# Scaling softmax probabilities on GpSimd instead of scaling the attention's output

## The reference, cut to what matters

```python
def attention(q, k, v, mask):
    scores = jnp.einsum('bhqd,bhkd->bhqk', q, k) / jnp.sqrt(jnp.float32(HD))
    scores = scores * mask - 10000.0 * (1.0 - mask)
    probs = jax.nn.softmax(scores, axis=-1)
    return jnp.einsum('bhqk,bhkd->bhqd', probs, v)
```

## Time and profile before

| What | Value |
|---|---|
| Median of 3 runs | 1197.53 us |
| The profiled execution's own time | 1199.37 us |
| Its span | 1197.6 us |
| TensorE busy (matmuls) | 1178.5 us, 98% |
| VectorE busy | 942.7 us, 79% |
| ScalarE busy | 849.1 us, 71% |
| GpSimd busy | 608.6 us, 51% |
| Granted TensorE clock, mean | 0.997 |

### The profile page before, as it was taken

One profiled execution on the slowest core, in us unless ns is written; L12 is line 12 of the kernel. 1 busy time (PEld: TensorE's weight loads), 2 busy tenths in 40 slices (PEclk: granted clock), 3 DMA queues, 4 the chain that ended last, 5 costly groups with the idle time before them and its releaser, 6 DMA issues.

```text
span 1197.6 us, 35319 instructions
## 1 busy us (share of the span) xinstructions
PE 1178.5 (98%) x13184; PEld 974.1 (81%) x13184; DVE 942.7 (79%) x2298; ACT 849.1 (71%) x2277; POOL 608.6 (51%) x1003
## 2 busy tenths in 40 slices
PE   9999999999999999999999999999999999999998
PEld 8778788787887878788788887878888787888877
DVE  4787887978788697787978788697887879779764
ACT  4777687767867778686767877677786786866543
POOL 3554664646455463654646455473654645363341
PEclk8999999999999999999999999999999999999999
DMA  8401000100100000010000100000000100000000
GB/s 238 142 33 31 2 24 1 31 2 16 33 6 27 5 14 19 11 30 5 24 1 2 44 6 23 8 15 2 22 28 2 31 13 6 8 6 2 1 7 10
DMA packets 27623, 27.91 MB, mean 23 GB/s; under 512 B 11072, under 2 KB 25408, under 8 KB 26816
## 3 DMA queue, kind: packets, MB, share of 16 engines
q1 hardware_dynamic: 26240, 24.99, 6.9%
q10 hardware_dynamic: 1216, 0.66, 0.3%
HBM read 23.53 MB, written 2.10 MB: 21 GB/s over the span
## 4 chain that ended last, share of the span: by engine, by line
PE 88%; DVE 4%; issue 3%; POOL 2%; ACT 2%; DMA 1%; SPq 0%; POOLq 0%; DVEq 0%; ACTq 0%
PE bank L659 10%; PE bank L539 9%; PE bank L932 9%; PE attended L614 9%; PE bank L942 9%; PE bank L599 9%; PE bank L694 6%; PE bank L665 5%; PE bank L720 4%; PE bank L683 4%; PE bank L707 4%; PE bank L652 3%; PE bank L510 2%; PE bank L433 2%; PE bank L711 2%
## 5 line engine op out<-in xcount | busy, mean ns | idle before, releaser
L586 POOL TENSOR_SCALAR p_a<-p_a,rec_a 128x256 f32<-128x256 f32 x512 | 245.9, 498 | 93.2 <-DVE rec_a L560 92.7
L575 ACT ACTIVATE p_a<-bank,nmax_a 128x256 f32<-128x256 f32 x512 | 237.6, 475 | 67.9 <-DVE nmax_a L554 66.8
L554 DVE TENSOR_REDUCE nmax_a<-bank 128x2 f32<-128x512 f32 x256 | 170.5, 680 | 24.0 <-PE bank L539 23.0
L599 PE MATMUL bank<-ident,p_a 128*128 128x128 f32 x1024 | 142.2, 274 | 0.3
L539 PE MATMUL bank<-cc,q_a 64*128 64x256 f32 x1024 | 133.4, 391 | 1.1 <-issue 0.2
L599 PEld LDWEIGHTS bank<-ident,p_a 128*128 128x128 f32 x1024 | 117.0, 141 | 13.2 <-issue 8.0
L614 PE MATMUL attended<-p_a,v_a 128*64 128x256 f32 x1024 | 125.2, 386 | 0.0
L539 PEld LDWEIGHTS bank<-cc,q_a 64*128 64x128 f32 x1024 | 94.7, 186 | 29.1 <-issue 15.2
L575 ACT ACTIVATION_READ_ACCUMULATOR p_a<-bank,nmax_a 128x1 f32 x512 | 104.9, 205 | 0.0
L614 PEld LDWEIGHTS attended<-p_a,v_a 128*64 128x64 f32 x1024 | 67.4, 136 | 41.5 <-issue 11.3
L632 DVE COPY p_a<-bank 128x512 f32<-128x512 f32 x128 | 86.3, 679 | 6.2 <-PE bank L599 5.5
(11 more groups left out here) (265 smaller groups left out, 2855.4 us busy)
## 6 DMA issues: line engine op xcount, KB each, us to landing
xx<-in_x SPq DMA_DIRECT2D x32, 128.0 KB, 3.0
cc<-in_ctx SPq DMA_DIRECT2D x32, 128.0 KB, 2.9
wc<-in_wc SPq DMA_DIRECT2D x3, 1024.0 KB, 7.3
k_c<-in_ctx SPq DMA_DIRECT2D x16, 128.0 KB, 2.3
wb<-in_wb SPq DMA_DIRECT2D x2, 1024.0 KB, 8.5
res_a<-in_x SPq DMA_DIRECT2D x16, 128.0 KB, 2.1
out<-y_out SPq DMA_DIRECT2D x16, 128.0 KB, 1.7
wb<-in_wb SPq DMA_DIRECT2D x2, 512.0 KB, 5.8
```

The costliest lines, as they stand in the source:

```text
L554: dve.tensor_reduce(nmax_a[:, n, e, :], ps[:, :].rearrange("p (q k) -> p q k", q=KT), AX.X, ALU.max, negate=True).then_inc(A.s["max"], 1)
L575: last = act.activation(p_a[:, j % 2, n, e, qt, :], ps[:, qt * D:(qt + 1) * D], ACT.Exp, bias=nmax_a[:, n, e, qt:qt + 1], accum_out=sum_a[ ...
L586: last = pool.tensor_scalar(p_a[:, j % 2, n, e, qt, :], p_a[:, j % 2, n, e, qt, :], rec_a[:, n, e, qt:qt + 1], 1.0, ALU.mult, ALU.mult)
L599: last = nc.tensor.transpose(ps[:, kt * D + qt * P:kt * D + (qt + 1) * P], p_a[:, j % 2, n, e, qt, kt * P:(kt + 1) * P], ident[:, :])
```

## The change

The reciprocals are applied to the probabilities before they are transposed. `pool_wide`, the tile `wide`, TensorE's two transposes of it and VectorE's multiply of `yT` go. `pool_scale` comes in their place: for each half r it multiplies `T.p` in place by the broadcast reciprocal. TensorE's transposes of the probabilities wait for this multiply instead of the exponential, ScalarE's copy waits for the transposes alone, and ScalarE's copy of fill "o" to `yT` releases the bank. The five order strings and `BANK` are new as a whole; the number of steps changes only by what was removed (VectorE's one step per attention, 64 in all) and by 13 steps of filler: WARM_UP is 29 for 17, IDLE_WORK 64 for 63.

```diff
-WARM_UP = 17
-IDLE_WORK = 63
+WARM_UP = 29
+IDLE_WORK = 64
...
-        "wwwwwwwwwwwwwwwwskwnsnksqqnanakkksaadskddkdkddnadadnsddsdaddaaddddqddqaaddkdkddnanabddkbddbdddnaaddbdbddbaanbdd"
+        "wwwwwwwwwwwwwwwwwwwwwwwwwwwnswwnkssqqnnksaakkkknksdaaddkdndddaaddkdddsdaaqdddsddqaaddddkddnanadbdkbnddbdddddaa"
...
-            T.wide = T.qT
...
-                    pe.wait_ge(T.s["exp"], T.at(i, "exp", r + 1))
+                    pe.wait_ge(T.s["scaled"], T.at(i, "scaled", r + 1))
                     ps = fill_bank(T, pe, i, ("t", r, c))
...
-            pe.wait_ge(T.s["wide"], T.at(i, "wide", KT))
-            for f in range(KT):
-                last = pe.transpose(ps[:, D + f * P:D + (f + 1) * P], T.wide[:, f, :], ident[:, :])
             filled(T, last, i, "o")
...
-            dve.wait_ge(T.s["att"], T.at(i, "att", 1))
-            ps = wait_fill(T, dve, i, "o")
-            ins = dve.tensor_tensor(T.yT[:, :, :], T.yT[:, :, :], ps[:, D:2 * D].rearrange("p (f q) -> p f q", q=P), ALU.mult)
-            release(T, ins, i, "o")
-            yield
...
-                    act.wait_ge(T.s["sum"], T.at(i, "sum", r + 1))
...
-            act.activation(T.yT[:, :, :], ps[:, 0:D].rearrange("p (f q) -> p f q", q=P), ACT.Copy).then_inc(T.s["att"], 1)
+            release(T, act.activation(T.yT[:, :, :], ps[:, 0:D].rearrange("p (f q) -> p f q", q=P), ACT.Copy), i, "o")
...
-        def pool_wide(T, i):
+        def pool_scale(T, i):
             pool = nc.gpsimd
-            for f in range(KT):
-                yield
-                pool.wait_ge(T.s["rec"], T.at(i, "rec", KT))
-                if i:
-                    written(T, pool, i - 1, "o")
-                heads = T.rec[:, :, :].rearrange("p r (g f e) -> p (r g) f e", g=QUADS // KT, f=KT)[:, :, f, :]
-                pool.tensor_copy(T.wide[:, f, :].rearrange("p (n e d) -> p n e d", n=QUADS, e=2), bc(heads, 3, HD)).then_inc(T.s["wide"], 1)
+            for r in range(KT):
+                yield
+                pool.wait_ge(T.s["rec"], T.at(i, "rec", r + 1))
+                v = heads_of(T, r)
+                pool.tensor_tensor(v, v, bc(bc(T.rec[:, r, :], 2, S), 1, T.blocks), ALU.mult).then_inc(T.s["scaled"], 1)
```

More of the change, by code:

```diff
@@ L161 @@
[L161 to L168 removed]
+        "wwwwwwwwwwwwwwwwwwwwwwwwwwwnswwnkssqqnnksaakkkknksdaaddkdndddaaddkdddsdaaqdddsddqaaddddkddnanadbkdnbddbdddddaa"
@@ new lines @@
+        "beanefbefnaafdgfkdkgkggkgkhbdknhckhccbdcnbddcbaaddbdkhhdeddaacecdecddcdeedddfdqqddfddfnneeeebaeaebffafkgdfkkgk"
+        "gbadkkhddgghhcbkcccbddcaabdhdkhcdcbdcddecaaefedfdfddeddedddfdffkkkddkbkbfeebeekehehhgbbgbgbgegeekeechcckchwcww"
+        "wwweewweewweweccwwcgcgggfgfwwfwwwwcwwwcccwwwcwffwwfwfwwwwwwwccwwchchwwfkfwwfhhhwwwwwffwwfwfwwwwwwwwwwwhwwwhhhh"),
+    "act": (
+        "sqknqqkqnsaakaadkadakaadadaaadkaadqqaaqqaddakaananabdabdadbdbaaadbbabaeadkaaeqqqqddeeaaneeeebaaenbadkgadbggbbd"
+        "aabbcaaedaacccdaadeccacaqdqqfdqeaaennbeeefebfaeffadfkkkagdakggaahbkcbhbchbabaddaccaedcacacadaeqfddeqeqnqeebeef"
+        "aaefnafdbfafagakggkdkaahkabdcabhkdhbcbbaacceadacacadceqfqddeeaqqbeeenfbefaeffnafdkkakagadgkhgaackbbchdbhbdabac"
+        "acaeacacdcadaeqfdqdeqeqnbeaeabefenfeadffafgaakkkggakhcbdbahbbchbadcakcedccaacaaddaafeddqeqqeqanbeefeefbaeffafa"
+        "kkdkagankaghgbabdbchdbcbdhcaackaaeacaccdadaefddeqeqnaeaeeefaefbqqbffdnafgakkgdkgacbhkkahhabcadbbdabacdcaeaacca"
+        "cadeqfqddeaeaqqbneeeefafneaffbadfkkkgdaggaahkcdbbaadhbbchbaaccdeaacccaadkfddeeeqqqqnfeeeefnaeabffbafdkakgkaagg"
+        "ahdcbbkakbcbhhbaadcecdccaacaadadaefddeeqnqqqeeefefaneffabfkakgbakadagdgabhacbkhbhbkcbaaddaeccaaaccdacdaefddqeq"
+        "eqnqeeeeffnebaafbfaafdkgakkaagdgbakhbcbhkbcbhaacdcdccaaceaadadafeddeqqeeaqneabeenfefqbdaafffagakkkgdgaahkbcbdb"
+        "dcbhhbakaacaecacacacddafdedeeqqqqeeeebfafenabffaanfadgkagkkgaahbcbdhkbkcbhbaadaccdaecacacddaafeqdqdeqeqnneeeeb"
+        "ffeaabffafagdkkkaagkgahbbdcakbcbhhadaccbccdacaeaafadadfefdffdfkkkebebkeeeeehbbgbbhbggehkeceeceeeececcccgggfcff"
+        "cfffccccchfhkhfffffhhh"),
@@ new lines @@
+    "pool": (
+        "snksaakaaaanaaaaaakkkaaaaaaaaaaaaabbknaaaeaeaagaeeeeaaaagabkabccaecaaccgaaancceaaaffaeekfekefaffaagahhkccaabba"
+        "caccaanceacaekaffaagaeefeefkfafagaakhahckacaababccncaceacakeaaffaaeekgefefffkaagahahaakcccnbbaccaaackacaaeaeff"
+        "agaeekkeffeafafgaahhkaccnbabcackceaaaccaaefafaaaeefkeefffgkaagakahhbcacbaacaccnakcaacageaeffaaaeeeeffkakaffgaa"
+        "kchhcakaacabbccacancaeaeafafaaeefkekefafafgagahaakhcacabbcnaccaagkcecaeaaffaaeeffeekkffaagakhhccabaacbnaackcec"
+        "acaaaeffaaaaeeffegeffkgaakaakhhccbkbcanaaccaacaaceaaaefgfaaeekefefffkaagakahhaccabbcakcaccaecnaaafaeafaaeeeeff"
+        "akfafgkgahhaaakccabbcanccaakccaaaeeffagaaeeefeffkfaagakahhakccbbacaccnaakgacaaecaeffaaaefefkfkfgaahkaahccbabca"
+        "akacccacaaffgaaaeeffakafkfekehhgbbekcgeccececccgffccffcffcccchhffkffffhh"),
@@ L189, in fill_places @@
+    "56130245062410563241506320421546320154360215436102536105236105246310524063124316321463214632146231462314623145"
+    "2631452631056431052643")
 def fill_places():
@@ L225 @@
 NORM = {"stats": 1, "mv": 1, "eps": 1, "rstd": 1, "xn": 1}
-SOFTMAX = {"kblk": 1, "max": KT, "sub": KT, "exp": KT, "sum": KT, "rec": KT, "wide": KT, "att": 1}
+SOFTMAX = {"kblk": 1, "max": KT, "sub": KT, "exp": KT, "sum": KT, "rec": KT, "scaled": KT}
 RAISED_K = {"c_in": 16, **NORM}
@@ L1116, in pool_e @@
                     nc.gpsimd.tensor_tensor(v, v, bc(bc(E.max[:, r, :], 2, S), 1, E.blocks), ALU.subtract).then_inc(E.s["sub"], 1)
-            yield from pool_wide(E, i)
+            yield from pool_scale(E, i)
         def pool_g(i):
@@ L1162, in pool_c @@
             yield from pool_attention(C, i, self_add, lambda pool: ready(pool, i))
-            yield from pool_wide(C, i)
+            yield from pool_scale(C, i)
         def pe_f(i):
@@ L1218, in pool_f @@
             yield from pool_attention(F, i, m4_add, lambda pool: pool.wait_ge(F.s["mask"], F.at(i, "mask", 2)))
-            yield from pool_wide(F, i)
+            yield from pool_scale(F, i)
         def pool_h(i):
```

119 lines of the change are left out of this document (47 added, 72 removed).

## The result

The changed kernel takes **1270.78 us** (median of 4 runs, 1268.34 to 1273.09) against 1197.81 us for the kernel before on the same chip: a ratio of 1.0611, 95% interval 1.0595 to 1.0628. It is 73 us slower where 10 us faster were forecast, and the time lies far outside the range.

What follows compares the result with a forecast made beforehand. TensorE, busy 893.4 of 900 us in the middle, was taken as the bound, with latency deciding near the end. The terms -13.8 + 1 + 4.0 - 2 = -10.8 us led to 1187 us, range 1182 to 1193.

Steps and rivals of the forecast that it cites:

- TensorE's work removed: Fill "o" loses its two transposes of `wide`: 60 fills at 0.23 us, 13.8 us off (12.0 to 17.4).
- The wait moved: TensorE's transposes wait for sum, reciprocal and multiply instead of the exponential: +1 us of new idle, between -4 and +9.
- The second: Rival: each attention's transposes wait on average 0.2 us for the multiply, eating the gain: 1198 us, chance 0.10.
- The third: Rival: GpSimd's queue runs late, TensorE stands at L599 about 1.2 us a pair: 1205 us, chance 0.14.
- 62% is far from full: Argument against the slower rival: GpSimd, forecast busy some 731 us or 62% of the span, has room.
- GpSimd's terms: New multiplies of 1.04 and 1.90 us less the spreading copy: +123 us, busy some 731 us, hidden behind TensorE.
- The tail: The last pair's stages, all on the chain, gain sum, reciprocal and multiply: +4.0 us (0 to +7).
- The start: Longer filler keeps TensorE's clock at the 2.4 GHz level: 2 us off, bounds -3.5 and +2.
- The shared port: VectorE's two-input SBUF subtractions and GpSimd's multiplies hold each other only now and then: a few us, the sum stays.
- rival 4: Clock still falls at the start, and subtractions of 0.68 us hold the last multiplies: -4 us, 1194 us, chance 0.07.

Runs made afterwards that it cites:

- e1: The changed kernel with the new multiply left out, TensorE's transposes waiting for the reciprocal, probabilities not normalised: 1188.46 us, ratio 0.9922 to the kernel before.
- e8: The changed kernel with the multiply in attention E alone; B, C and F wait for the reciprocal and are not normalised: 1240.55 us, ratio 1.0353.
- e5: The changed kernel with another order of GpSimd's steps alone, other orders, banks and instructions unchanged: 1251.07 us, ratio 1.0443.
- e2: The changed kernel with the multiply on 2 of the 8 heads of each half, the others undivided: 1194.66 us, ratio 0.9968.
- e4: The kernel before with 29 filler matmuls at the start in place of 17, nothing else: 1198.99 us, ratio 1.0012.
- e10: The changed kernel with all orders and banks laid out anew, TensorE's changes of stationary shape counted as a cost: 1230.98 us, ratio 1.0279.
- e11: The kernel before with all orders and banks laid out anew in the way of e10: 1219.3 us, ratio 1.0177.
- e7: The kernel before with all orders and banks laid out anew, changes of stationary shape not priced: 1270.04 us, ratio 1.0609.
- e9: The kernel before with 384 matmuls added at TensorE's end on ready weights, alternating two stationary shapes in groups of 32, 4 and 1: 1391.58 us, one run.
- e12: The changed kernel with the multiply done by VectorE right behind the reciprocal in place of GpSimd, orders and banks kept: 1280.97 us, ratio 1.0697.
- e3: The changed kernel with E's subtraction of the maximum for pairs 0 to 12 moved from GpSimd to VectorE: 1296.92 us, ratio 1.0822.

## Why the prediction was wrong

**TensorE's work removed (-13.8).** Supported, not shown alone: e1 has the removed transposes, the new orders and the longer filler, and gains 9.3 us against the kernel before. The sign was right; how the 9.3 us divide was not measured.

**"The wait moved", +1 us, bounds -4 to +9.** This is the step that failed. I found 1 to 3 us more of other TensorE work between scores and transposes in the new string and called it "about what the new path needs". The path's own additions, by the prediction's figures, are 0.66 + 0.19 + 1.04 + 0.15 = 2.04 us in B, C and F and 1.20 + 0.19 + 1.90 + 0.15 = 3.4 us in E, before any queue. An average over four stages set against an average need hides the stages that are short. By the trace of e1 the order leaves 1.11 us for E's multiply of 1.95 and 0.66 us for F's of 1.04; in B and C the averages suffice, and a third to nearly a half of the halves are short even so. E is where 43.4 of the 81.0 us of idle are (the group e_p L811), and e8, with the multiply in E alone, loses 52 us. The term measured 60 us between the first and last x1, and 69 with the 9 us that e1 shows to be gained there.

**Rivals.** The second (each attention waits 0.2 us) was right in place and six times too small: 81.0 us over 64 attentions is 1.27 us each. The third was right that GpSimd's queue runs late, which e5 prices at 20 us, and wrong in place (L599: 5.5 us) and size. "62% is far from full" was no argument: with GpSimd busy 643 us e8 loses 52 us, with 631 us e2 loses 6. A share of busy time says nothing on whether one step at one place is in time.

**GpSimd's terms.** Multiplies 1.04 and 1.95 us (forecast 1.04 and 1.90), busy 737 us (731): right, and of no use to the result, since the sum took their cover for granted.

**The tail (+4).** What follows the last x1 grew by 10.0 us. In e1 it is 108.2 us against 108.9, so all of it is the multiply's; the term was too small by 6. This part comes back in both pairs of replanned orders (6.7 and 7.5 us): one pair's stages stand in a row there, and the multiply is one more piece in it.

**The start (-2).** The clock stayed at 1.00 from 12 to 18 us, as forecast, where it had been 0.50, the 1.2 GHz level. The first x1 came 1.0 us sooner, half of the 2 us. The filler alone doesn't do it: in e4 the clock still fell, at 16.6 us, the first q matmul came at 16.0 us and the first x1 0.2 us later than before. In the changed kernel the first q matmul comes at 15.1 us for 14.1; that this delay ate the other half is argued, not shown.

**The shared port (rival 4).** F's subtraction had 639/691/812 ns (min/median/max) before and a mean near the median. After:

```profile
L749 DVE TENSOR_TENSOR f_p<-f_p,f_max x32: 660/706/2396, 163.4 to 1245.4; 128x512 f32<-128x512 f32 x32
```

The median barely moves, the longest is 2.4 us, and the mean is 992 ns, 302 more than before, 9.7 us over 32. The trace shows why the two differ. 18 of the 32 subtractions began while GpSimd was inside a TENSOR_TENSOR of 512 or 1024 columns, 11 of them in E's new multiply; each of these took what was left of GpSimd's instruction and 0.55 us more. The other 14 took 0.69 us on average and never more than 0.71. In the kernel before 7 began beside such an instruction, at most 0.27 us before its end. So the prediction misread its rows: the medians stay near 0.69 us because few subtractions before, and only about half of F's now, have such a neighbour, not because one beside it often goes free. The rule on the port that it cited (the Trainium skill, SBUF — State Buffer, "Who interferes with whom") agrees with this trace. The 9.7 us lie on F's path ahead of the exponential, and what they add to the run's time was not measured by itself.

**What stays open.** Whether an order exists that hides the multiply altogether. e10 leaves 33 us over the kernel before, of which its control e11 has 21 without any multiply, so these seem to belong to my replanning. Two pairs of orders that put the change at -4 and +12 us don't fix what it costs at its best. Of e7's 72 us some 23 are more than e9's price for the changes of shape; whether a change costs more among real steps than in e9, or steps stand too close behind what they wait for, is not shown. No version that computes the whole beat the kernel before; e1's 9 us are what the changed kernel gains where its multiply is free.

## What to carry to other kernels

When a wait moves to a later event, don't compare average slack with average need: for each stage take the time between the two TensorE steps in the written order and set it against the sum of that stage's own path, and take the worst. Busy share is not slack; a step on an engine that is half idle can cost most of its length, on whichever engine it stands. Judge an edit together with an order laid out for it: here the same edit costs 73 us in the orders that it came with, and -4 and +12 us in two pairs of orders laid out in one way for both kernels.

## What the runs showed of the hardware that was not expected

- A change of the stationary tile's shape on TensorE (whole, 64 rows, 64 columns) costs 0.19 and 0.17 us (e9, one run), shows as "issue", and is in no wait. By this price the 219 fewer changes of e11 are an estimated 42 of the 51 us between e7 and e11, whose orders differ in more than that.
- GpSimd's multiply with a broadcast factor takes 1.04 us for 512 columns and 1.90 for 1024 (medians; E's mean is 1.95); its addition of a mask broadcast over the heads takes 1.29 for 512. VectorE's multiply of the same operands took 0.71 to 0.80 and 1.41 us on average (e12), with medians of 0.69 and 1.23.
- A VectorE subtraction with both inputs in SBUF that began inside a GpSimd TENSOR_TENSOR of 512 or 1024 columns ended 0.55 us after that one's end, in 18 of 18 cases (F, changed kernel); without such a neighbour it took 0.69 us.
- Waits of TensorE inside a full kernel can bring the granted clock down: it was 1.00 throughout e1, and 0.50 for 17 us of the changed kernel, 31 of e8 and 41 of e3. Past the first 15 us each fall came behind a stretch in which TensorE had stood idle for a good part, as in the rows shown.
